# Sixteen-head values turned by VectorE's block transposes, and self-attention with scores 32 keys wide, in a two-layer latent transformer kernel

## The chip, the cores and the metric

The kernel runs on one core of a Trainium2 chip. The metric is the device time of one execution in microseconds; lower is better. The engines are named as in the profile: PE is TensorE's matrix multiplication and PEld its loading of weights, DVE is VectorE, ACT is ScalarE, POOL is GpSimd, SP is SyncE. Each has its own instruction queue and works it off in order; an instruction waits at the head of its queue until the semaphores that it needs have come up, and everything behind it waits too.

## The reference, cut to what matters

The input x has 128 sequences of 32 tokens with 256 features, and each sequence has a context of 257 rows. Six blocks follow one another, each of the form x = x + f(layernorm(x)):

```python
x = x + _L0_xattn_ref(_layernorm(x), ctx_1024, ...)   # one head, 257 context keys
x = x + _L0_attn_ref(_layernorm(x), ...)              # one head of 128, causal over the 32 tokens
x = x + _L0_ffn_ref(_layernorm(x), ...)               # quantised feed-forward, 256 -> 1024 -> 256
x = x + _L1_xattn_ref(_layernorm(x), ctx_1024, ...)   # 16 heads of 16, 257 context keys
x = x + _L1_attn_ref(_layernorm(x), ...)              # tokens at most 2 away
x = x + _L1_ffn_ref(_layernorm(x), ...)               # 8 experts, the best 2 for each token
```

Three of them matter here. The sixteen-head cross attention computes, for each sequence, softmax(q k) v for 16 heads with 32 queries and 257 keys, and multiplies the concatenated heads by an output matrix. The two self-attentions (causal in layer 0, a band of five tokens in layer 1) only ever combine tokens of one sequence of 32.

## The kernel before

A tile is 128 rows, that is four sequences of 32 tokens; there are 32 tiles. The first phase takes each tile through all six blocks up to the router. It is software-pipelined: a slot of the program holds, on each engine, the steps of up to nine tiles at different depths (`slot(s)` in each engine's block, with `at(s + 3, ...)` for a tile that is three behind in depth), and the order of the steps in a slot is written out by hand for every engine. The second phase runs the experts: 71 blocks of 128 gathered rows, each with 2 x 8 products up and 8 down. Some closing steps of the last two tiles stand between the first expert blocks.

The sixteen-head attention is the largest part of a slot. A unit is one sequence of a tile, so a slot has four units. For a unit, PE writes scores into PSUM banks 0 to 3 (`unit_scores`, L1246), DVE takes row maxima (`unit_max`, L1797), ACT takes exponentials and row sums (`unit_probs`, L1431), PE transposes the probabilities in the same four banks (`unit_probs_T`, L1254), ACT copies them out (L1435), and PE multiplies by the context (`values_of`, L1265) into bank `V{u}`. The next unit's scores wait for that copy, since they use the same banks. The rows of the V bank are (head within half, query), and its 64 columns hold four groups of 16 features.

What follows the values is the part that the change replaces. DVE adds the last key's product (`unit_own`, L825), then multiplies by a 0/1 selection of two halves that carries the reciprocal of the row sum (L827, 128 columns wide; the selection comes from POOL, `unit_select`, L1562). PE folds the rows with a constant matrix (`unit_fold`, L729), which also turns features to partitions. DVE copies the result from PSUM to the tile's transposed output (`unit_folded`, L832). `s1_out` multiplies that by the output matrix.

In both self-attentions PE computes scores for 128 queries against all 128 keys of a tile, and a mask 128 wide removes the keys of other sequences (`masked_max`, L812 and L814). ACT takes the exponential; PE transposes the probabilities (`s0_probs_T` L1178, `s1_probs_T` L777); ACT copies them out (L1387, L896); PE multiplies by the values (`s0_values` L1182, `s1_values` L782). In layer 0, DVE divides by the row sum ahead of the transpose (L1733). In layer 1 this is done behind the values (`s1_x5`, L863).

Two helpers of the waits appear below: `W_bank` names the last readers of the PSUM bank that a product is about to overwrite, and `f1_ok` counts units whose folded values are ready.

## Time and profile before

| quantity | value |
|---|---|
| median of 3 runs | 1440.78 us (1439.78 to 1440.86) |
| the profiled execution | 1438.83 us |
| span of its trace | 1436.9 us |
| granted TensorE clock, mean over the span | 0.989 |
| PE busy | 1383.0 us, 96% |
| PEld busy | 1181.8 us, 82% |
| DVE busy | 892.7 us, 62% |
| ACT busy | 839.2 us, 58% |
| POOL busy | 642.2 us, 45% |

The shares are averages over two phases with different limits: in the first, three engines are busy nearly all the time; in the second, DVE and ACT have little to do. Matmuls are pipelined and their ends are modelled, so records of PE overlap; the same holds for DVE and ACT, where an instruction's record can start before the one ahead has ended. The time that an instruction costs its queue is read from start to start.

### The profile page before, as it was taken

The numbers are of one execution on the slowest core, as the hardware profiler recorded it, in microseconds if no ns is written. First come the engines' busy times: TensorE is split into PE (matmuls) and PEld (weight loads), VectorE is DVE, ScalarE is ACT, GpSimd is POOL, SyncE is SP. The second block draws the span as 40 slices with busy tenths as digits, with TensorE's granted clock in tenths as the row PEclk, the third lists the DMA queues.
The fourth block names the chain that finished last, engine by engine and source line by source line (L and its number), as shares of the span: only waits on it lengthen the run. The fifth ranks groups of instructions, "written<-read, shape, count | busy, mean of one in ns | idle before, by whom it ended". The sixth has DMA issues, their size and how long they took to land. (4 is left out here: it accounts for less than half of the span.)

```text
span 1436.9 us, 51496 instructions
## 1 busy us (share of the span) xinstructions
PE 1383.0 (96%) x19614; PEld 1181.8 (82%) x19647; DVE 892.7 (62%) x3143; ACT 839.2 (58%) x2431; POOL 642.2 (45%) x1195
## 2 busy tenths in 40 slices
PE   8789999999999999999999988999999999999996
PEld 6467788878878788888887866899999999999996
DVE  5678989999999999999999985333111111111111
ACT  1588989889888898889888875331111111111110
POOL 1233444434455455454554543366544434444442
PEclk9899999999999999999999999999999999999999
DMA  9423433334334334343332233666666666665662
GB/s 326 152 72 95 123 105 106 119 94 117 105 113 116 102 102 120 107 121 101 105 113 87 62 130 114 227 177 180 180 182 182 191 183 182 181 182 178 181 181 58
DMA packets 91181, 199.49 MB, mean 139 GB/s; under 512 B 13568, under 2 KB 48128, under 8 KB 79840
## 3 DMA queue, kind: packets, MB, share of 16 engines
q1 hardware_dynamic: 72304, 174.68, 38.3%
q0 software_dynamic: 15680, 18.69, 7.3%
q10 hardware_dynamic: 2992, 3.28, 0.7%
q8 instruction: 141, 2.31, 0.6%
q14 instruction: 64, 0.52, 0.1%
HBM read 178.58 MB, written 18.29 MB: 137 GB/s over the span
## 5 line engine op out<-in xcount | busy, mean ns | idle before, releaser
L2177 ACT ACTIVATE heT<-ps 128x512 f32<-128x512 f32 x142 | 84.8, 598 | 411.9 <-PE ps L2099 382.7
L2099 PEld LDWEIGHTS ps<-xeT,w_block 128*128 128x128 f32 x2272 | 264.8, 192 | 3.6 <-issue 0.2
L2099 PE MATMUL ps<-xeT,w_block 128*128 128x128 f32 x2272 | 266.2, 275 | 0.0
L1431 ACT ACTIVATE x_prob<-ps,x_nmax 128x257 f32<-128x257 f32 x512 | 237.5, 473 | 46.5 <-DVE x_nmax L1797 41.9
L2086 PE MATMUL ps<-contexts,heT 128*128 x1136 | 257.6, 379 | 1.6 <-DVE ye L1984 1.6
L2086 PEld LDWEIGHTS ps<-contexts,heT 128*128 128x128 f32 x1136 | 210.1, 190 | 27.6 <-issue 1.9
L1797 DVE TENSOR_REDUCE x_nmax<-ps 128x2 f32<-128x514 f32 x256 | 169.0, 681 | 18.9 <-PE ps L1246 18.6
L1983 DVE COPY to_ix<-places 128x1 uint32 x71 | 10.9, 154 | 231.8 <-PE ps L2086 228.2
L1254 PE MATMUL ps<-constants,x_prob 128*128 128x128 f32 x1024 | 150.1, 280 | 4.3 <-ACT x_prob L1431 4.1
L1435 ACT ACTIVATE x_probT<-ps 128x512 f32<-128x512 f32 x256 | 148.2, 632 | 3.6 <-PE ps L1254 3.3
L2220 POOL TENSOR_TENSOR rt_hold<-constants 128x1 f32<-128x1 f32 x143 | 35.0, 244 | 227.2 <-DVE ye L1984 121.0
L1254 PEld LDWEIGHTS ps<-constants,x_prob 128*128 128x128 f32 x1024 | 115.5, 143 | 19.2 <-ACT x_prob L1431 14.0
L2226 POOL DMA_INDIRECT out<-ye,to_ix x71 | 113.0, 1592 | 28.5 <-issue 23.8
L1265 PEld LDWEIGHTS ps<-contexts,x_probT 128*32 128x32 f32 x8192 | 90.5, 110 | 31.4 <-ACT ffn_hidden L1400 11.8
L1431 ACT ACTIVATION_READ_ACCUMULATOR x_prob<-ps,x_nmax 128x1 f32 x512 | 103.2, 202 | 0.0
L1265 PE MATMUL ps<-contexts,x_probT 128*32 128x16 f32 x8192 | 93.9, 185 | 6.3 <-issue 5.9
L1246 PE MATMUL ps<-contexts,query_blocks 32*64 32x257 f32 x2048 | 89.4, 405 | 6.8 <-ACT x_probT L1435 4.8
L2002 DVE COPY xeT<-ps 128x256 f32<-128x256 f32 x71 | 30.1, 424 | 85.0 <-PE ps L2077 85.0
L2223 POOL DMA_INDIRECT xe<-xnorm,from_ix x69 | 69.2, 1003 | 22.5 <-issue 20.4
L1562 POOL TENSOR_TENSOR x_select<-constants,x_rinv 128x8 f32<-128x8 f32 x128 | 27.5, 215 | 107.7 <-DVE x_rinv L1801 107.7
L1557 POOL TENSOR_TENSOR x_lastv<-contexts,x_prob 128x64 f32<-128x64 f32 x128 | 40.6, 317 | 55.5 <-ACT x_prob L1431 55.0
L1246 PEld LDWEIGHTS ps<-contexts,query_blocks 32*64 32x64 f32 x2048 | 30.3, 131 | 41.9 <-ACT x_probT L1435 25.1
(287 smaller groups left out, 2940.2 us busy)
## 6 DMA issues: line engine op xcount, KB each, us to landing
w_block<-in_m_w SPq DMA_DIRECT2D x71, 1024.0 KB
contexts<-in_cT SPq DMA_DIRECT2D x112, 257.0 KB
contexts<-in_cn SPq DMA_DIRECT2D x112, 256.0 KB
contexts<-in_m_w SPq DMA_DIRECT2D x8, 1024.0 KB
contexts<-in_cT SPq DMA_DIRECT2D x4, 1028.0 KB
xin<-in_x SPq DMA_DIRECT2D x32, 128.0 KB, 2.1
lastq<-in_lastq SPq DMA_DIRECT2D x32, 128.0 KB, 2.2
contexts<-in_cn SPq DMA_DIRECT2D x4, 1024.0 KB
```

Of the source, the lines that this page charges most:

```text
L1246: i = mm(ps[h * HS:(h + 1) * HS, r, 0:KEYS], qblk[t % 2][r * GD:(r + 1) * GD, h, u, :, :].rearrange("p e q -> p (e q)"), cT[t % RING][r * ...
L1254: i = tr(ps[:, r, n * P:(n + 1) * P], p1[u % 2][:, r, n * P:(n + 1) * P], ident[:])
L1265: i = mm(b[rows_of, r * DH:(r + 1) * DH], p1T[u % 2][:, r, n, rows_of], cn[t % RING][:, u, n, lo:lo + DH], start=n == 0, stop=n == KT - 1)
L1431: A(p1[u % 2][:, r, :], ps[:, r, 0:KEYS], ACT.Exp, bias=nmax1[u % 2][:, r:r + 1], accum_out=rsum1[u % 2][:, r:r + 1]).then_inc(e1_ok.handl ...
L1435: A(p1T[u % 2][:, 2 * j:2 * j + 2].rearrange("p r k t -> p r (k t)"), ps[:, 2 * j:2 * j + 2, 0:KT * P], ACT.Copy).then_inc(t1_ok.handle, 1)
L1557: tt(lastv[u % 2][:].rearrange("p (r d) -> p r d", r=RG), lastk[t % RING][:, u, :].rearrange("p (r d) -> p r d", r=RG), p1[u % 2][:, :, KE ...
L1797: v_.tensor_reduce(nmax1[u % 2][:, 2 * j:2 * j + 2], ps[:, 2 * j:2 * j + 2, 0:KEYS], AX, ALU.max, negate=True).then_inc(m1_ok.handle, 1)
L2086: t = mm(ps[:, 3, 0:D], heT[b][:, k, :], w2[:, e, k, :], start=k == 0, stop=k == FK - 1)
L2099: t = mm(ps[:, half, at:at + P], w1[b][:, k, f * P:(f + 1) * P], xeT[b][:, k, :], start=k == 0, stop=k == H - 1)
L2177: A(heT[b][:, half * FK // 2:(half + 1) * FK // 2, :].rearrange("p k t -> p (k t)"), ps[:, half, :], ACT.Gelu).then_inc(heT_ok.handle, 1)
L2223: g.indirect_dma_start(xe[b][:], None, sources[round_of(u, n)], bass.IndirectOffsetOnAxis(ap=from_ix[b][:], axis=0)).then_inc(xe_in[b], 16)
L2226: g.indirect_dma_start(sums[round_of(u, n)], bass.IndirectOffsetOnAxis(ap=to_ix[b][:], axis=0), ye[b][:], None, compute_op=ALU.add).then_i ...
```

## The change

It has four parts.

1. Values of the sixteen heads. The columns of the value weights are put in another order on the host (`x1_wv`), so that 32x32 blocks turned in place give the wanted layout. The selection, the product with it and the fold are gone. DVE adds the last key (`unit_own`), POOL divides by the row sum (`unit_scaled`, 128x64), and DVE turns the 32x32 blocks of the result into the transposed output (`unit_turned`, one transpose, 128x64). `unit_values` of units 1 and 3 wait for other readers of their banks than before, since the fold's banks are no longer used.
2. Layer 0 self-attention. PE computes four 32x32 score products instead of one of 128x128. The mask, maximum and exponential are 32 columns wide. DVE multiplies by the reciprocal of the row sum and spreads the 32 columns over 128 under a block mask in one instruction, and turns the 32x32 blocks with a transpose of 128x128. PE's transpose and ACT's copy are gone.
3. Layer 1 self-attention. Eight 32x32 score products instead of two of 128x128, and again mask, maximum and exponential 32 wide. DVE turns the 128x32 probabilities and spreads them under the block mask (`s1_turned`). PE's transpose and ACT's copy are gone. `s1_out` now stands ahead of `s1_values` on PE.
4. Order. On POOL the steps `unit_scaled` stand near where `unit_select` stood, with the changes shown below.

The core of the diff:

```diff
         def s1_out(t):
             W(pe, f1_ok, t, NB)
-            W_bank(pe, (t - 1, (act_s["self1"], "probsT")))
...
-            product(bank(B["s1_v_scores"])[:, D:D + P], [(q1T[:, k, :], xnT["self1"][:, k, :]) for k in range(H)]).then_inc(pe_s["self1"].handle, 1)
-
-        def s1_probs_T(t):
-            W(pe, act_s["self1"], t, "probs")
-            W_bank(pe, (t + 1, (f1_ok, 3)))
-            tr(bank(B["s1_probs_T"])[:, 0:P], prob["self1"][:], ident[:]).then_inc(pe_s["self1"].handle, 1)
+            for k in range(H):
+                for b in range(NB):
+                    i = mm(bank(B["s1_v_scores"])[b * S:(b + 1) * S, D:D + S], q1T[:, k, b * S:(b + 1) * S], xnT["self1"][:, k, b * S:(b + 1) * S], start=k == 0, stop=k == H - 1)
+            i.then_inc(pe_s["self1"].handle, 1)
...
             W(dve, v1_ps, t, u + 1)
-            W(dve, sel_ok, t, u + 1)
+            W(dve, lv_ok, t, u + 1)
+            W_if(dve, before[0], n1_ok, before[1] + 1)
             v_.tensor_tensor(own[q][:], bank(B[f"V{u}"])[:, 0:OWN], lastv[q][:], ALU.add).then_inc(o1_ok.handle, 1)
-            W(dve, o1_ok, t, u + 1)
-            v_.tensor_tensor(om[q][:], own[q][:].rearrange("p (r d) -> p r d", r=RG).unsqueeze(1).broadcast_to([P, H, RG, DH]),
-                             select[q][:].unsqueeze(3).broadcast_to([P, H, RG, DH]), ALU.mult).then_inc(om_ok.handle, 1)
-
-        def unit_folded(t, u):
-            W(dve, f1_ps, t, u + 1)
-            v_.tensor_copy(outT[t % 2][:, :, u * S:(u + 1) * S], bank(B[f"f{u}"])[:, 0:HS].rearrange("p (e q) -> p e q", e=HG)).then_inc(f1_ok.handle, 1)
+
+        def unit_turned(t, u):
+            W(dve, n1_ok, t, u + 1)
+            v_.transpose(outT[t % 2][:, :, u * S:(u + 1) * S], scaled[u % 2][:].rearrange("p (j c) -> p j c", j=H)).then_inc(f1_ok.handle, 1)
...
+        def s1_turned(t):
+            W(dve, act_s["self1"], t, "probs")
+            v_.transpose(turned[:], prob["self1"][:]).then_inc(dve_s["self1"].handle, 1)
+            W(dve, dve_s["self1"], t, "turned")
+            v_.tensor_tensor(in_blocks(probT["self1"][:, 0, :]), turned[:].unsqueeze(1).broadcast_to([P, NB, S]), in_blocks(const["blocks"]), ALU.mult).then_inc(dve_s["self1"].handle, 1)
...
+        def unit_scaled(t, u):
+
+            q = u % 2
+            before = unit_before(t, u, 2)
+            W_if(pool, before[0], f1_ok, before[1] + 1)
+            W(pool, r1_ok, t, u + 1)
+            W(pool, o1_ok, t, u + 1)
+            tt(scaled[q][:].rearrange("p (r d) -> p r d", r=RG), own[q][:].rearrange("p (r d) -> p r d", r=RG),
+               rinv1[q][:].unsqueeze(2).broadcast_to([P, RG, DH]), ALU.mult).then_inc(n1_ok.handle, 1)
...
                 W(dve, dve_s["self0"], t, "inv")
-                v_.tensor_scalar(prob["self0"][:], prob["self0"][:], rinv["self0"][:], None, ALU.mult).then_inc(dve_s["self0"].handle, 1)
+                v_.scalar_tensor_tensor(in_blocks(spread[:]), prob["self0"][:].unsqueeze(1).broadcast_to([P, NB, S]), rinv["self0"][:], in_blocks(const["blocks"]), ALU.mult, ALU.mult).then_inc(dve_s["self0"].handle, 1)
+                W(dve, dve_s["self0"], t, "scaled")
+                v_.transpose(probT["self0"][:, 0, :], spread[:]).then_inc(dve_s["self0"].handle, 1)
```

The first place is on VectorE (DVE) in the last part of a slot, from the third unit's turned values to the row maxima of the next tile's second unit. The row `rt_rest` belongs to the router, `ffn_hidden` and `ffn_hq` to the feed-forward of another tile. Before:

```order
L832 COPY x1_outT<-ps 128x2x32
L812 SCALAR_TENSOR_TENSOR self1_masked<-ps,constants 128x128
L814 TENSOR_REDUCE self1_nmax<-self1_masked 128x1
L1760 TENSOR_SCALAR ffn_hidden<-ffn_hidden,ffn_qscale 128x1024
L1762 TENSOR_SCALAR ffn_hq<-ffn_hidden 128x1024
L1797 TENSOR_REDUCE x1_nmax1<-ps 128x2
L832 COPY x1_outT<-ps 128x2x32
L273 SCALAR_TENSOR_TENSOR rt_rest<-rt_hot,rt_shifted 128x32
L1797 TENSOR_REDUCE x1_nmax1<-ps 128x2
L818 RECIPROCAL self1_rinv<-self1_rsum 128x1
```

And now:

```order
L816 STREAM_TRANSPOSE x1_outT<-x1_scaled0 128x2x32
L797 SCALAR_TENSOR_TENSOR self1_masked<-ps,constants 128x32
L799 TENSOR_REDUCE self1_nmax<-self1_masked 128x1
L1742 TENSOR_SCALAR ffn_hidden<-ffn_hidden,ffn_qscale 128x1024
L1744 TENSOR_SCALAR ffn_hq<-ffn_hidden 128x1024
L1780 TENSOR_REDUCE x1_nmax1<-ps 128x2
L816 STREAM_TRANSPOSE x1_outT<-x1_scaled1 128x2x32
L843 STREAM_TRANSPOSE self1_prob_turned<-self1_prob 128x32
L845 TENSOR_TENSOR self1_probT<-self1_prob_turned,constants 128x128
L273 SCALAR_TENSOR_TENSOR rt_rest<-rt_hot,rt_shifted 128x32
L1780 TENSOR_REDUCE x1_nmax1<-ps 128x2
L803 RECIPROCAL self1_rinv<-self1_rsum 128x1
```

The two copies from PSUM have become transposes in SBUF, the mask is narrower, and two instructions have come in ahead of the second row maximum.

The second place is on GpSimd, at about the same time, from the bias of one tile to the reciprocal deviation of the layer 1 self-attention. Before:

```order
L915 TENSOR_TENSOR self0_x_bias<-x1_0,r_a0_bo 128x256
L1562 TENSOR_TENSOR x1_select1<-constants,x1_rinv1 128x8
L1557 TENSOR_TENSOR x1_lastv0<-contexts,x1_prob 128x64
L915 TENSOR_TENSOR x3_bias<-x3,r_x1_bo 128x256
L915 TENSOR_TENSOR self1_x_bias<-x4,r_a1_bv 128x256
L909 TENSOR_TENSOR router_var_eps<-router_moments,epsilon 128x1
L911 TENSOR_TENSOR router_rstd<-router_var_eps,minus_half 128x1
L1562 TENSOR_TENSOR x1_select0<-constants,x1_rinv0 128x8
L915 TENSOR_TENSOR cross0_x_bias<-xin3,r_x0_bv 128x256
L1557 TENSOR_TENSOR x1_lastv1<-contexts,x1_prob 128x64
```

And now:

```order
L904 TENSOR_TENSOR self0_x_bias<-x1_0,r_a0_bo 128x256
L924 TENSOR_TENSOR x1_scaled0<-x1_own0,x1_rinv0 128x64
L924 TENSOR_TENSOR x1_scaled1<-x1_own1,x1_rinv1 128x64
L1542 TENSOR_TENSOR x1_lastv0<-contexts,x1_prob 128x64
L904 TENSOR_TENSOR x3_bias<-x3,r_x1_bo 128x256
L904 TENSOR_TENSOR self1_x_bias<-x4,r_a1_bv 128x256
L898 TENSOR_TENSOR router_var_eps<-router_moments,epsilon 128x1
L900 TENSOR_TENSOR router_rstd<-router_var_eps,minus_half 128x1
L904 TENSOR_TENSOR cross0_x_bias<-xin3,r_x0_bv 128x256
L1542 TENSOR_TENSOR x1_lastv1<-contexts,x1_prob 128x64
```

Two products 128x64 stand where one of 128x8 stood, and the bias `cross0_x_bias` follows the router's `router_rstd` with nothing between them.

The third place is on TensorE, from the next tile's second scores to the hidden transposes of the feed-forward. Before:

```order
L1246 MATMUL ps<-contexts,query_blocks1 64x257 x8
L729 MATMUL ps<-constants,x1_own_half1 128x64
L777 MATMUL ps<-constants,self1_prob 128x128
L709 MATMUL ps<-self0_normT,w_a0_Wq_T 128x128 x2
L709 MATMUL ps<-self0_normT,w_a0_Wk_T 128x128 x2
L709 MATMUL ps<-w_a0_Wv_T,self0_normT 128x128 x2
L782 MATMUL ps<-self1_val,self1_probT 128x256
L709 MATMUL ps<-x1_W,x1_outT 128x128 x4
L1254 MATMUL ps<-constants,x1_prob 128x128 x8
```

And now:

```order
L1243 MATMUL ps<-contexts,query_blocks1 64x257 x8
L711 MATMUL ps<-self0_normT,w_a0_Wq_T 128x128 x2
L711 MATMUL ps<-self0_normT,w_a0_Wk_T 128x128 x2
L711 MATMUL ps<-w_a0_Wv_T,self0_normT 128x128 x2
L711 MATMUL ps<-x1_W,x1_outT 128x128 x4
L767 MATMUL ps<-self1_val,self1_probT 128x256
L1251 MATMUL ps<-constants,x1_prob 128x128 x8
```

The fold and the transpose are gone, and the output product has moved ahead of the values of the self-attention.

## Rows read from the trace of the kernel before

**Rows 1.** Windows of the trace: stretch, length, busy time and instructions per engine, clock, DMA
```profile
112.90:839.40 726.50, 715.63 (x13905) 582.67 (x13933) 671.50 (x2336) 645.40 (x1985) 353.47 (x763) 1.00 0.36 107
910.00:1437.00 527.00, 515.07 (x3543) 484.01 (x3541) 106.16 (x444) 92.34 (x153) 232.08 (x305) 0.99 0.61 172
```

**Rows 2.** DVE groups from 112.9 to 839.4 us: busy us, mean ns, idle before
```profile
L832 DVE COPY x_outT<-ps 128x64 f32<-128x64 f32 x112 | 24.6, 220 | 7.4 <-PE ps L729 7.2
L812 DVE SCALAR_TENSOR_TENSOR self_masked<-ps,constants 128x128 f32<-128x128 f32 x56 | 16.3, 290 | 5.7 <-issue 2.4 <-ACT self_val L888 2.3 <-PE ps L1173 0.6
L814 DVE TENSOR_REDUCE self_nmax<-self_masked 128x1 f32<-128x128 f32 x56 | 16.0, 286 | 1.9
L1733 DVE TENSOR_SCALAR self_prob<-self_prob,self_rinv 128x128 f32<-128x128 f32 x28 | 8.3, 295 | 1.0
L273 DVE SCALAR_TENSOR_TENSOR rt_rest<-rt_hot,rt_shifted 128x32 f32<-128x32 f32 x6 | 1.1, 182 | 0.0
L263 DVE TENSOR_REDUCE rt_top<-rt_key 128x4 f32<-128x32 f32 x6 | 1.1, 180 | 0.0
```

**Rows 3.** Waits from 112.9 to 839.4 us: total us, times, longest
```profile
POOL x_lastv L1557 <- ACT x_prob L1431: 40.0, 13, 3.6
ACT query_normT L1415 <- PE ps L1226: 32.2, 28, 1.2
ACT x_prob L1431 <- DVE x_nmax L1797: 31.7, 56, 1.2
PEld ps L1246 <- ACT x_probT L1435: 19.9, 59, 0.9
DVE x_nmax L1797 <- PE ps L1246: 10.6, 30, 0.4
DVE x_outT L832 <- PE ps L729: 7.2, 28, 0.7
```

**Rows 4.** DVE timeline, the fourth unit's addition and product: start, duration in us
```profile
407.22 0.22 DVE L825 TENSOR_TENSOR x_own<-ps,x_lastv 128x64 f32<-128x64 f32 x1
407.47 0.29 DVE L827 TENSOR_TENSOR x_own_half<-x_own,x_select 128x128 f32<-128x128 f32 x1
407.68 1.21 DVE L1750 TENSOR_REDUCE ffn_absmax<-ffn_hidden 128x1 f32<-128x1024 f32 x1
```

**Rows 5.** PE timeline around a fold, a change of tile shape and score products
```profile
404.00 0.33 PE L729 MATMUL ps<-constants,x_own_half 128*128 128x64 f32 x2
404.16 0.59 PE L709 MATMUL ps<-f,ffn_xqT 128*128 128x512 bf16 x2
404.69 0.69 PE L1246 MATMUL ps<-contexts,query_blocks 32*64 32x257 f32 x16
411.66 0.28 PE L777 MATMUL ps<-constants,self_prob 128*128 128x128 f32 x1
411.78 0.61 PE L709 MATMUL ps<-self_normT,w_a_Wq_T 128*128 128x128 f32 x4
416.75 0.47 PE L1173 MATMUL ps<-self_kT,self_qT 128*128 128x128 f32 x2
417.15 0.69 PE L1246 MATMUL ps<-contexts,query_blocks 32*64 32x257 f32 x16
```

**Rows 6.** ACT timeline around one of the two copies that go
```profile
420.59 0.29 ACT L1387 ACTIVATE self_probT<-ps 128x128 f32<-128x128 f32 x1
420.75 0.50 ACT L1431 ACTIVATE x_prob<-ps,x_nmax 128x257 f32<-128x257 f32 x1
```

**Rows 7.** Timelines of POOL and DVE, where work of both overlaps
```profile
414.92 0.82 POOL L915 TENSOR_TENSOR cross_x_bias<-xin,r_x_bv 128x256 f32<-128x256 f32 x1
415.18 0.60 DVE L288 TENSOR_TENSOR rt_key<-rt_key,constants 128x32 f32<-128x32 f32 x1
```

**Rows 8.** DVE timeline: the first unit's addition, and its copy after the fold
```profile
419.90 0.22 DVE L825 TENSOR_TENSOR x_own<-ps,x_lastv 128x64 f32<-128x64 f32 x1
422.25 0.23 DVE L832 COPY x_outT<-ps 128x64 f32<-128x64 f32 x1 [0.19 <-PE ps L729]
```

More of the change, by code:

```diff
@@ L544, in stack_phase @@
     val = {n: small(n, "val", D) for n in ATT[1:]}
-    masked = {n: small(n, "masked", P) for n in ATT[1:]}
+    masked = {n: small(n, "masked", S) for n in ATT[1:]}
+    spread = small("self0", "prob_spread", P)
+    turned = small("self1", "prob_turned", S)
     nmax = {n: small(n, "nmax") for n in ATT}
@@ L602, in stack_phase @@
         "cross0": ["normT", "q", "scores", "probsT", "values", "attT", "out"],
-        "self0": ["normT", "qkv", "scores", "probsT", "values", "out"],
+        "self0": ["normT", "qkv", "scores", "values", "out"],
         "ffn_in": ["inT"],
@@ L695, in at @@
         name = step.__name__
-        left = CLOSING.get(name, int(name in ("unit_own", "unit_fold", "unit_folded") and unit[0] >= 2))
+        left = CLOSING.get(name, int(name in ("unit_own", "unit_scaled", "unit_turned") and unit[0] >= 2))
         if 0 <= t < tiles - left:
@@ L1084, in setup_folds @@
                 t.then_inc(su_mm, 1)
[L1086 removed]
+            product, product_in_halves, route_counts, W_counts, s1_out, s1_norm_T, s1_q, s1_v_scores, s1_values, ro_norm_T, ro_logits = tensor_steps(pe)
             def c0_norm_T(t):
@@ L2030, in _ @@
             unit_own(tiles - 1, 3)
-            unit_folded(tiles - 1, 2)
+            unit_turned(tiles - 1, 2)
             s1_masked(tiles - 2)
-            unit_folded(tiles - 1, 3)
+            unit_turned(tiles - 1, 3)
             stage_from(2, 0)
+            s1_turned(tiles - 2)
             s1_inv(tiles - 2)
@@ L2048, in _ @@
             s1_masked(tiles - 1)
+            s1_turned(tiles - 1)
             s1_inv(tiles - 1)
@@ L2070, in _ @@
             mm = nc.tensor.matmul
-            product, product_in_halves, unit_fold, route_counts, W_counts, s1_out, s1_norm_T, s1_q, s1_v_scores, s1_probs_T, s1_values, ro_norm_T, ro_logits = tensor_steps(pe)
+            product, product_in_halves, route_counts, W_counts, s1_out, s1_norm_T, s1_q, s1_v_scores, s1_values, ro_norm_T, ro_logits = tensor_steps(pe)
             def rows_T(u, b):
```

160 lines of the change are left out of this document (67 added, 93 removed), and 3 rows, old and new, of the table B.

## The prediction, on record before the change was run

> **What bounds the kernel now.** I read the windows first, because the page's shares mix two phases. The stretch from 112.9 to 839.4 us [rows 1] holds 28 slots: the copy L832 has 112 records there, four in a slot [rows 2]. So a slot takes 726.5 / 28 = 25.95 us. Busy in it: PE 98%, DVE 92%, ACT 89%, POOL 49%. The last 527 us are the experts, where DVE and ACT are busy for a fifth of the time and PE for 98%. The change touches nothing of an expert block, so that stretch keeps its length whatever happens ahead of it.
>
> The waits of the same stretch come second [rows 3]. Per slot, DVE waits 10.6 / 28 = 0.38 us for PE's scores and 7.2 / 28 = 0.26 us for the fold; together about 0.6 us of 26. ACT waits 2.3 us, for PE's query transposes and DVE's maxima. PE waits 0.7 us for ACT's copies. The reader is to see a ring: scores on PE, maxima on DVE, exponentials on ACT, transposes on PE, copies on ACT, and then the next unit's scores in the same banks. Steps of other tiles fill each queue in between. DVE has the least slack, PE little more, ACT the most. So a shorter DVE queue is worth the most, as long as PE's shrinks as much and ACT can give up enough of its 2.3 us.
>
> **The change, part by part.** Costs of DVE are from start to start.
>
> *Units.* In [rows 4] the addition starts at 407.22, the product with the selection at 407.47, the next instruction at 407.68: 0.25 + 0.21 us. The 0.25 contains the wait for the addition's own result. An instruction that nobody waits for overlaps the next by 0.08 us (0.29 long, 0.21 to the next start), so alone the addition costs 0.22 - 0.08 = 0.14. Four units: 4 x (0.46 - 0.14) = 1.28 us less in a slot.
>
> *Transposes.* No row of before has one on DVE. I price them like a product. SCALAR_TENSOR_TENSOR takes 182 ns for 32 columns and 290 for 128 [rows 2], so about 1.1 ns a column and 217 ns for 64, against 220 for the PSUM copy that goes. The four `unit_turned` then cost nothing net. A slot transposes 416 columns (4 x 64 + 128 + 32). From below I bound them by half that slope, since an instruction with one input might stream faster: 0.23 us less. From above by double the slope: 0.46 us more. I take the middle, to which all rows of products are nearest. The Trainium skill (VectorE: DVE Perf Modes, The three transpose paths) gives 311 ns for 128x128 in bf16; by it the sum would be 0.02 us longer per slot. No row here shows it.
>
> *Narrow masks.* Mask and maximum go from 290 and 286 to 182 and 180 ns [rows 2]: 0.21 us, for two self-attentions 0.43 us less.
>
> *Layer 0 spread and transpose.* The product 128x128 (295 ns [rows 2], 0.21 to the next start) becomes a product with two inputs (0.29 + 0.03 for the wait behind it) and a transpose (0.21): 0.32 us more.
>
> *Layer 1 turn.* Transpose 128x32 (0.18 + 0.03) and product 128x128 (0.21): 0.42 us more, ahead of the second row maximum of the next unit, for which ACT's exponentials wait.
>
> DVE's sum is -1.28 - 0.43 + 0.32 + 0.42 = -0.97 us a slot.
>
> *PE.* A fold takes 0.16 us of the queue (404.00 to 404.16 [rows 5]), four 0.64. A transpose takes 0.12 (411.66 to 411.78), two 0.24. The layer 0 scores take 0.40 from start to the next product (416.75 to 417.15), those of layer 1, twice the records of the same shape at 0.11 to 0.12 each, about 0.44. The new ones are 8 and 16 records of 32 columns into four groups of output partitions. Sixteen records of 257 columns in small tiles need 0.62 us of queue at most (0.69 long [rows 5]), so the new ones get 0.1 and 0.2. A change of tile shape costs too: of the two L709 records at 404.16 the second starts 0.22 later, at 404.38, and L1246 starts at 404.69, 0.31 behind it instead of 0.22. That is 0.09 us for a change; layer 0 adds one and layer 1 two. The new scores take about 0.2 and 0.4 instead of 0.84. PE's sum: -0.64 - 0.24 - 0.24 = -1.1 us a slot, so PE follows DVE.
>
> The Trainium skill (TensorEngine Tiling (Array Packing), Key Properties) says that changing the tiling mode drains TensorE, which speaks against the small products. The trace shows a drain at 0.09 us. Were it a whole record (0.28) three times, PE's sum would be -0.55, and PE would set the slot at 0.4 us less than now instead of 0.9.
>
> *ACT.* A copy costs 0.16 us (420.59 to 420.75 [rows 6]). Two go, and two exponentials lose 96 columns, by DVE's slope 0.1 us each: -0.5. To follow DVE, ACT gives up 0.4 of its 2.3 us of waiting.
>
> *POOL.* Four products 128x64 replace four of 128x8. Here the trace speaks against the change. At 414.92 POOL starts a bias, and DVE's 32-column product at 415.18 takes 0.60 us [rows 7], where such a product takes 0.18 [rows 2]: 0.4 us lost. The new order puts that bias right behind the router's deviation, so that it can fall on layer 1's turn, which works in SBUF; and POOL's product for the second unit can fall on the normalisation behind that unit's addition. I bound this by 0 (no overlap) and 0.8 us (both hit) a slot and take 0.3. The Trainium skill (GPSIMD Engine Reference, Specifications) says that the SBUF interfaces are shared with VectorE, with contention for two-input and two-port instructions; the trace agrees.
>
> POOL's wait for the additions of the last two units stands where it waited for exponentials before (40.0 / 13 = 3.1 us each time [rows 3]), so what is behind it in the queue is not later. The closest pair of addition and turned unit on DVE is 2.35 us apart (419.90 and 422.25 [rows 8]), against a product of POOL of well under 1 us. No new wait.
>
> *Moved products.* `s1_out` now runs ahead of `s1_values`, so `s1_x5` gets its values about an output product later, and `s1_x` its sum earlier. DVE has the turn, a maximum of 0.6 us and a normalisation between. No cost.
>
> **The sum.** DVE -0.97, the wait for the fold -0.26, contention +0.3: 0.9 us a slot, 28 slots, 25 us. Ahead of 112.9 and behind 839.4 us lie parts of about four more slots, which I price at 0.75 us each: 3 us. Against the profiled execution 1438.8 - 28 = 1410.6 us. It lies 1.95 us below the median of the runs, so against the median 1412.5 us.
>
> **The rivals.** The forecast, 0.9 us a slot, has a chance of 0.49.
>
> First, more: ring and queues close up together, so that ACT's and PE's savings count beside DVE's and nothing collides. With the bound of no contention DVE alone gives 0.97 + 0.26 = 1.23 us a slot: 1440.8 - 35 - 4 = 1402 us. For it: all three engines wait for one another in [rows 3]. Against it: their savings lie beside each other in time as often as behind each other. Chance 0.2.
>
> Second, less, from DVE: transposes at their upper bound (+0.46) and contention at its own (0.8 instead of 0.3) leave nothing of the 0.9; halfway, at 0.4 us a slot, it is 1440.8 - 11 - 2 = 1428 us. For it: the 0.60 in [rows 7]. Against it: the additions that go were as exposed as the products that come. Chance 0.15.
>
> Third, less, from ACT: its queue loses only 0.5 us, and if its waits are latency of the ring and not slack, the slot loses no more than that: 1440.8 - 14 - 2 = 1425 us. Against it: the waits are in two places of the slot and both are for engines that get shorter. Chance 0.1.
>
> Fourth, slower: a block transpose is dear. The 0.9 us are used up when each of the 416 columns costs 2.2 ns more than the 1.1, that is from 3.3 ns. At 5 ns it is 0.7 us more a slot, 1460 us. Against it: operations of quite different kinds have the same slope in [rows 2] (product 1.1, maximum 1.1). Chance 0.04.
>
> Fifth, no change: DVE's queue is shorter, but what arrives sets the pace. The 0.6 us that DVE waits now would then grow to 1.5 a slot. Against it: PE at 98% loses 1.1 us too. Chance 0.02.
>
> **How the numbers follow.** The range takes in the first three rivals with the bounds of what they price: 1396 to 1431 (from 1.4 to 0.3 us a slot). A measurement of this kernel can tell 0.2% (2.9 us) from no change. Faster: the forecast and the first three rivals, 0.94. Same: the fifth, 0.02. Slower: the fourth, 0.04.
>
> **What would show it.** In the changed kernel's trace: the spacing of unit scores four apart is near 25.0 us; transposes 128x64 take 200 to 250 ns and 128x128 about 290; the narrow masks 180; there is no wait of DVE for a fold; the new layer 0 scores take PE under 0.3 us; DVE's normalisation behind the second unit's addition stays at 0.41 or doubles (contention); ACT's waits shrink by 0.4 us a slot. The prediction is wrong if the transposes' slope is above 2 ns a column, if POOL's bias stretches the 128x128 product beyond 0.5 us, or if a new wait for POOL's scaled values shows up on DVE.

## The result, and the profile after

The changed kernel is slower: 1457.21 us median of 4 runs (1453.08 to 1459.9) against 1440.82 us (1439.78 to 1443.4), ratio 1.0106 with a 95% interval of [1.0081, 1.013]. Its profiled execution took 1456.48 us. The head of its page, and the row of the queue that brings PE's instructions (packets, MB, share):

```profile
span 1454.7 us, 51945 instructions
PE 1365.7 (94%) x19870; PEld 1136.4 (78%) x19903; DVE 870.6 (60%) x3111; ACT 823.6 (57%) x2367; POOL 653.1 (45%) x1195
q8 instruction: 142, 2.33, 0.6%
```

Every engine but POOL is busy for less time than before, and the span is 17.8 us longer. What went must have come back as waiting. Windows of the changed kernel, from the start of a slot (unit 3's scores, L1243) to the start of another, columns as in [rows 1]:

```profile
139.40:267.40 128.00, 124.17 (x2519) 95.23 (x2524) 114.21 (x379) 111.92 (x344) 58.87 (x131) 1.00 0.38 110
423.00:749.60 326.60, 303.32 (x6072) 234.91 (x6084) 282.00 (x1006) 271.87 (x831) 165.64 (x339) 0.99 0.34 104
749.60:855.30 105.70, 98.99 (x2003) 75.53 (x2007) 95.56 (x351) 89.83 (x271) 54.03 (x109) 1.00 0.29 94
```

And of the kernel before, the same slots:

```profile
138.40:266.40 128.00, 127.09 (x2479) 103.32 (x2484) 116.27 (x385) 114.79 (x354) 57.36 (x130) 1.00 0.37 110
422.90:734.00 311.10, 307.55 (x5977) 251.06 (x5989) 289.73 (x1018) 277.56 (x855) 161.36 (x340) 1.00 0.37 110
734.00:839.40 105.40, 102.17 (x1973) 82.44 (x1977) 97.80 (x356) 91.55 (x279) 54.21 (x111) 1.00 0.29 94
```

The reader is to see two results. Slots 2 to 6 (128.0 us, five slots) are exactly as long as before, 25.60 us each: no gain where nothing disturbs. Slots 13 to 24 (twelve slots) took 311.1 us and take 326.6: a loss of 15.5 us, nearly the whole difference. The rest of the balance: start +1.2, the other early slots -1.1, slots 25 to 28 +0.3, the last two slots +3.5, what is behind -1.6; together 17.8 us.

The operations of the change on DVE, as groups from 112.9 to 839.4 us (busy us, mean ns | idle before):

```profile
L816 DVE STREAM_TRANSPOSE x_outT<-x_scaled 128x64 f32<-128x64 f32 x110 | 25.3, 230 | 0.0
L812 DVE TENSOR_TENSOR x_own<-ps,x_lastv 128x64 f32<-128x64 f32 x111 | 21.2, 206 | 6.9 <-PE ps L1262 6.8
L845 DVE TENSOR_TENSOR self_probT<-self_prob_turned,constants 128x128 f32<-128x128 f32 x27 | 13.9, 513 | 0.9
L797 DVE SCALAR_TENSOR_TENSOR self_masked<-ps,constants 128x32 f32<-128x32 f32 x54 | 10.2, 189 | 33.3 <-ACT self_val L881 18.1 <-issue 14.8
L1713 DVE SCALAR_TENSOR_TENSOR self_prob_spread<-self_prob,self_rinv,constants 128x128 f32<-128x128 f32 x27 | 9.5, 352 | 1.0
L1715 DVE STREAM_TRANSPOSE self_probT<-self_prob_spread 128x128 f32<-128x128 f32 x27 | 8.4, 312 | 0.9
```

The block transposes cost what the prediction gave them. The new thing is L797: DVE idles 33.3 us ahead of the narrow masks.

**A slot without a stall.** Waits of ACT from 139.4 to 267.4 us, five slots (total us, times, longest):

```profile
ACT x_prob L1418 <- DVE x_nmax L1780: 8.9, 15, 0.9
ACT query_normT L1402 <- PE ps L1223: 5.8, 5, 1.2
```

In the kernel before, from 138.4 to 266.4 us:

```profile
ACT query_normT L1415 <- PE ps L1226: 5.8, 5, 1.2
ACT x_prob L1431 <- DVE x_nmax L1797: 5.5, 10, 0.8
```

ACT's busy time fell by 2.87 us in these five slots (114.79 to 111.92), and its waiting rose by 3.4. Its queue runs through the whole slot with these waits alone. Where they come from is seen on DVE, in the slot that starts at 241.8 us:

```profile
254.75 0.19 DVE L797 SCALAR_TENSOR_TENSOR self_masked<-ps,constants 128x32 f32<-128x32 f32 x1 [0.82 <-ACT self_val L881]
254.98 0.19 DVE L799 TENSOR_REDUCE self_nmax<-self_masked 128x1 f32<-128x32 f32 x1
255.08 0.77 DVE L1742 TENSOR_SCALAR ffn_hidden<-ffn_hidden,ffn_qscale 128x1024 f32<-128x1024 f32 x1
255.88 1.10 DVE L1744 TENSOR_SCALAR ffn_hq<-ffn_hidden 128x1024 bf16<-128x1024 f32 x1
256.90 0.68 DVE L1780 TENSOR_REDUCE x_nmax<-ps 128x2 f32<-128x514 f32 x1
257.50 0.23 DVE L816 STREAM_TRANSPOSE x_outT<-x_scaled 128x64 f32<-128x64 f32 x1
257.66 0.16 DVE L843 STREAM_TRANSPOSE self_prob_turned<-self_prob 128x32 f32<-128x32 f32 x1
257.86 0.64 DVE L845 TENSOR_TENSOR self_probT<-self_prob_turned,constants 128x128 f32<-128x128 f32 x1
258.42 0.68 DVE L1780 TENSOR_REDUCE x_nmax<-ps 128x2 f32<-128x514 f32 x1
```

DVE reaches the mask early and waits 0.82 us for ACT's copy of layer 1's values, which stands where it stood before: the saving ahead of it is lost there. Behind it layer 1's turn (257.66 to 258.42, 0.76 us) stands ahead of the second row maximum, and ACT waits for that one too, 0.41 us, where it had waited once for this unit. The product of the turn takes 0.64 us with POOL's bias running beside it; in the slots where nothing 128x256 on POOL overlaps it, it takes 0.29:

```profile
257.62 0.73 POOL L904 TENSOR_TENSOR cross_x_bias<-xin,r_x_bv 128x256 f32<-128x256 f32 x1
```

Why ACT waits although it has work in its queue is seen at the start of a slot, here the one at 190.6 us:

```profile
189.91 0.64 ACT L1422 ACTIVATE x_probT<-ps 128x512 f32<-128x512 f32 x1
191.71 0.39 ACT L1402 ACTIVATE query_normT<-ps 128x256 f32<-128x256 f32 x1 [1.15 <-PE ps L1223]
```

PE's unit scores may start only behind this copy, at 190.61; they and the query transposes behind them take until ACT's next step. So the 1.15 us are the way from ACT's own copy through PE and back, and no shorter queue of DVE changes them.

**A slot with a stall.** PE in the slot that starts at 450.1 us, which takes 28.4 us:

```profile
458.54 1.29 PE L1262 MATMUL ps<-contexts,x_probT 128*32 128x16 f32 x125
461.48 0.24 PE L1262 MATMUL ps<-contexts,x_probT 128*32 128x16 f32 x3 [1.65 <-issue]
```

It stops three products before the end of the values products of units 2 and 3, and no semaphore holds it ("issue"). In the transfers from 459.0 to 460.3 us there is one packet of the instruction queue:

```profile
q8 instruction: 1, 0.02, 5.5%
```

The packet starts at 459.06 and takes 1.15 us; PE goes on at 461.48, 2.4 us behind its start. By the page, 142 such packets bring 2.33 MB, so PE's code comes in pieces of 16 KB. Counting PE's records in the trace (loads of weights, products, waits), I find one piece per 256 records. A slot has 1029 records in the trace of the changed kernel and 1020 in that of the kernel before, so the borders of the pieces move through the slot: earlier by 5 records from slot to slot in the one, later by 4 in the other, and some slots have 9 or 13 records more. I number them by the records ahead of a slot's start, modulo 256. In the changed kernel this count is 47 to 67 in slots 2 to 7, 72 to 102 in slots 8 to 12, and 107 to 192 in slots 13 to 24.

The clock is touched as well: behind two of the stalls in slots 13 to 24 (those that end at 490.0 and 572.5 us) the granted clock stood at the lower of its two levels, 1.2 GHz, for 3.4 us.

### The profile page after: what moved, and what is told of

Read it like the earlier page. It is cut to its first block and busy times, and to the rows that moved or that the text cites. A ratio compares the mean times of both kernels' runs of the same rounds, so it can differ in the third digit from the quotient of the medians.

```text
span 1454.7 us, 51945 instructions
## 1 busy us (share of the span) xinstructions
PE 1365.7 (94%) x19870; PEld 1136.4 (78%) x19903; DVE 870.6 (60%) x3111; ACT 823.6 (57%) x2367; POOL 653.1 (45%) x1195
## 3 DMA queue, kind: packets, MB, share of 16 engines
q8 instruction: 142, 2.33, 0.6%
## 5 line engine op out<-in xcount | busy, mean ns | idle before, releaser
L1251 PE MATMUL ps<-constants,x_prob 128*128 128x128 f32 x1024 | 157.6, 284 | 14.0 <-ACT x_prob L1418 12.3
L1422 ACT ACTIVATE x_probT<-ps 128x512 f32<-128x512 f32 x256 | 147.9, 626 | 11.1 <-PE ps L1251 10.0
L1251 PEld LDWEIGHTS ps<-constants,x_prob 128*128 128x128 f32 x1024 | 119.3, 145 | 34.9 <-ACT x_prob L1418 27.8
L2208 POOL DMA_INDIRECT out<-ye,to_ix x71 | 113.0, 1592 | 28.4 <-issue 23.9
L924 POOL TENSOR_TENSOR x_scaled<-x_own,x_rinv 128x64 f32<-128x64 f32 x128 | 37.0, 297 | 177.5 <-DVE x_own L812 169.1
L1243 PE MATMUL ps<-contexts,query_blocks 32*64 32x257 f32 x2048 | 89.0, 403 | 16.0 <-ACT x_probT L1422 13.8
L2205 POOL DMA_INDIRECT xe<-xnorm,from_ix x69 | 69.2, 1003 | 22.5 <-issue 20.3
L1243 PEld LDWEIGHTS ps<-contexts,query_blocks 32*64 32x64 f32 x2048 | 30.3, 130 | 50.1 <-ACT x_probT L1422 33.5
## 6 DMA issues: line engine op xcount, KB each, us to landing
contexts<-in_cn SPq DMA_DIRECT2D x112, 256.0 KB
xin<-in_x SPq DMA_DIRECT2D x32, 128.0 KB, 2.1
lastq<-in_lastq SPq DMA_DIRECT2D x32, 128.0 KB, 2.2
```

Source lines behind the costliest of these rows:

```text
L1243: i = mm(ps[h * HS:(h + 1) * HS, r, 0:KEYS], qblk[t % 2][r * GD:(r + 1) * GD, h, u, :, :].rearrange("p e q -> p (e q)"), cT[t % RING][r * ...
L1251: i = tr(ps[:, r, n * P:(n + 1) * P], p1[u % 2][:, r, n * P:(n + 1) * P], ident[:])
L1422: A(p1T[u % 2][:, 2 * j:2 * j + 2].rearrange("p r k t -> p r (k t)"), ps[:, 2 * j:2 * j + 2, 0:KT * P], ACT.Copy).then_inc(t1_ok.handle, 1)
L2205: g.indirect_dma_start(xe[b][:], None, sources[round_of(u, n)], bass.IndirectOffsetOnAxis(ap=from_ix[b][:], axis=0)).then_inc(xe_in[b], 16)
L2208: g.indirect_dma_start(sums[round_of(u, n)], bass.IndirectOffsetOnAxis(ap=to_ix[b][:], axis=0), ye[b][:], None, compute_op=ALU.add).then_i ...
```

## The experiments: does the place of PE's code matter?

Two theories stood after the comparison. A: pieces of code that come late at a bad place of the slot cost the 15 us. B: the change's own work does (POOL beside DVE, new waits). The test shifts the code by records that do nothing, ahead of the first tile, and leaves all else. Each ratio below is against the kernel before, timed beside the run; its median lies between 1440.8 and 1443.5 us from one group of runs to another, so runs of different groups are best compared by their ratios. The first form:

```diff
             keep_busy(13)
+            for _ in range(56):
+                mm(ps[:, 3, 0:1], zero[:, 0:P], zero[:, 0:1], start=True, stop=True)
```

**56 products in the changed kernel.** 

> The changed kernel with 56 extra products of one column (112 records on PE) ahead of the first tile, where PE waits for the first loads. Nothing else differs. Theory A: the 20 us that the changed kernel loses between 423 and 907 us come from where the boundaries of the loaded pieces of PE's code fall in a slot (one piece per 256 records, a slot has 1029). They then fall 112 records earlier in the program, the slots of 27 to 29 us go, and the time comes to 1432 to 1440 us. Theory B: the loss is the work itself (POOL's products beside DVE's, waits for the turned probabilities): the same as the changed kernel within 3 us, 1457.

1473.46 us, ratio 1.0216 [1.0193, 1.0238].

**96 products in the changed kernel.** 

> The changed kernel with 96 extra products of one column (192 records on PE) at the same place. Theory A: the first half of the tiles runs in slots of 25.6 to 26 us, the second half gets the stalls that the changed kernel has in slots 13 to 19, shifted to later slots: 1440 to 1455 us, with a stall inside the block of values products in other slots than before. Theory B: 1457 as the changed kernel.

1481.71 us, 1.029 [1.0256, 1.0325].

**72 products in the kernel before.** 

> The kernel before with 72 extra products of one column (144 records on PE) at the same place. Theory A: the kernel before has 1020 records in a slot, so its boundaries hardly move from slot to slot; the shift puts them where the changed kernel stalls, in nearly all slots: 1455 to 1490 us, slots of 26.5 to 28.5 us. Theory B: 1441 as before, within 3 us.

1461.29 us, 1.0135 [1.0118, 1.0152].

All three expectations missed, for two reasons that the traces show. Each product left four records on PE, not two, so the shifts were 224, 384 and 288 records. And the products delayed the first tile by 21, 36 and 28 us. With the delay set aside the slots are informative: in the kernel with 96 products slots 13 to 24 have counts of 235 to 255 and 4 to 64 and take 26.03 us each, against 27.22 without them; with 56 products the counts are 75 to 160 and they take 27.07.

The second form uses small products (64 by 16, four records each), 28 of them for 112 records:

```diff
+            for i in range(28):
+                mm(ps[i % H * HS:(i % H + 1) * HS, 3, 0:DH], zero[:, 0:HS], zero[:, 0:DH], start=True, stop=True)
```

**28 small products in the changed kernel.** 

> The changed kernel with 28 small products (64 by 16, of zeros, 112 records on PE) ahead of the first tile, so that PE's code is shifted by 112 records. The products of 128 by 1 of the first four runs had four records each and delayed the first tile by 21 to 36 us; these should delay it by less than 3. Theory A (pieces of PE's code come late where their boundary falls ahead of the values products): a slot that starts with 72 to 165 records (of 256, counted in the trace) is long, and this shift takes all slots but the last few out of that range: slots 13 to 24 of 25.6 to 26.2 us instead of 25.8 to 28.7, in all 12 to 20 us less than the changed kernel, 1437 to 1446 us. Theory B (work and contention): 1457 us plus the delay of the first tile.

1450.64 us, 1.0069 [1.0046, 1.0092]. Slots 13 to 24 take 26.03 us each, as expected; but slots 2 to 5, with counts of 159 to 169, take 28.0 to 29.5, so the bad range reached further than I had it. Not all of that is code: each of the four has a gap of 2.1 us from start to start, and at the end of each gap or up to 1.3 us behind it the granted clock fell to 1.2 GHz for 3.4 to 6.8 us (mean 0.92 from 142.4 to 256.0 us). What such a fall costs is seen in the next kernel, where one of the slots with a gap has it and takes 28.8 us, while the others up to slot 24 take 27.0 to 27.8.

**35 in the kernel before.** 

> The kernel before with 35 such products (140 records on PE), which by theory A puts all its slots from 3 to 28 into the long range: slots of 26.5 to 28 us instead of 25.7 to 26.3, and 1465 to 1490 us. Theory B: 1441 to 1445 us.

1479.39 us, 1.0277 [1.0235, 1.0318]: 38 us lost by 140 records that do nothing. Waits of PE from 439.8 to 767.8 us, slots 13 to 24:

```profile
PEld ps L1267 <- issue: 20.9, 12, 2.1
PE ps L1267 <- issue: 19.7, 12, 2.0
```

Each of the twelve slots stalls in the values products, about 1.7 us. In the whole run there are 26 such gaps, and PE goes on 2.2 to 2.8 us behind the start of a packet of code every time.

**32 in the changed kernel.** 

> The changed kernel with 32 small products of zeros (128 records on PE) ahead of the first tile: 16 records more than the kernel with 28. By the count of records at each slot's start, slots 2 to 5, which were 28 us long with 28 products, leave the long range, and slots 25 to 28 stay at its other edge. Theory A: 8 to 12 us less than with 28 products, 1438 to 1443 us, and slots 2 to 24 on average 25.9 us, as the kernel before. Rival: the long slots of a run are set by something else than the count, and the time stays at 1448 to 1452 us.

1446.87 us, 1.0035 [1.002, 1.0051]. One gap is left, in slot 3.

**8 in the kernel before.** 

> The kernel before with 8 such products (32 records on PE), by the same count its best place: slots 7 to 9 and 14 of 26.3 to 26.8 us become 25.7 us: 2 to 5 us less than before, 1436 to 1439 us. With it stands how the change compares at the best place of each: theory A gives a difference of less than 5 us between this kernel and the changed one with 32 products. Rival: no effect, 1441 us.

1435.09 us, 0.9954 [0.9936, 0.9973], with no such gap left. But it and the changed kernel are 11.8 us apart, not less than 5: this half of the expectation missed, and the end of the text comes back to it.

| kernel | count in slots 13 to 24 | mean slot, 13 to 24 |
|---|---|---|
| before, 8 small products | 27 to 37 | 25.88 us |
| before | 226 to 245 | 25.93 us |
| changed, 28 small products | 219 to 249, then 7 to 48 | 26.03 us |
| changed, 32 small products | 250, then 9 to 90 | 26.05 us |
| changed, 56 products | 75 to 160 | 27.07 us |
| changed | 107 to 192 | 27.22 us |
| before, 35 small products | 110 to 129 | 27.33 us |

Theory A holds, in both kernels and both directions: counts of about 100 to 170 cost 1.0 to 1.5 us a slot. The counts have one flaw. Most of the traces lack the record of one product in each slot (the changed kernel has 19,902 loads of weights and 19,870 products); in the table only the kernels with 32 and with 8 small products lack none, so in slots 13 to 24 the counts of the other rows are too low by 16 to 28. With this set right the gaps fall on one place: all 26 in the kernel with 35 small products, and all five of over 0.9 us in the values products of the changed kernel, stand 193 or 194 records behind a multiple of 256. A border of a piece does that; work and contention, which know nothing of such a count, would not. The Trainium skill (Runtime: NRT & Kernel Launch, Instruction fetch mechanics) says that code is fetched in 16 KiB blocks of 256 instructions and that crossing a boundary is mostly hidden. The trace agrees with the sizes; it doesn't agree that it is hidden here, where 256 records of the values products pass in 1.3 us and the next piece needs 2.2 us or more.

## The experiments: why no slot got shorter

**ReLU for GELU in the changed kernel with 32 small products.** It takes ACT's two table loads (1.28 us each) away and computes another function in the feed-forward. The second half of the hidden rows has the same edit.

```diff
-A(hid[:, 0:FF // 2], bank(B["ff_up0"]), ACT.Gelu, scale=dq[:, 0:1])
+A(hid[:, 0:FF // 2], bank(B["ff_up0"]), ACT.Relu, scale=dq[:, 0:1])
```

> a_code128 with ReLU in place of GELU in the feed-forward of the tiles, which takes two table loads of 1.28 us out of ACT's queue in each slot and nothing from another engine. Theory D (ACT's own queue, with the ring's latency where it waits, sets the slot, and DVE's and PE's savings lie in their slack): the slot shrinks by 0.5 us or more, up to DVE's queue: 24.3 to 25.3 us, 1400 to 1430 us. Rival (DVE sets the pace, as the prediction had it): ACT's waits grow by 2.5 us and the slot stays at 25.6 to 25.9 us, 1440 us.

1424.9 us, 0.9892 [0.9867, 0.9917]. Slots 4 to 7 take 24.78 us instead of 25.58. So 0.80 of the 2.56 us came back; the rest became waiting. In 102.3 us from 195.0 us on, ACT now waits 4.0 us for PE's products into the hidden rows, where it hadn't waited, and 10.6 us for the maxima instead of 7.1.

**The absolute maximum over 128 of 1024 columns, in the same kernel.** It takes 1 us from DVE and computes another scale.

```diff
-row_scale("ffn", t, 1, hid)
+row_scale("ffn", t, 1, hid[:, 0:P])
```

> a_code128 with the absolute maximum of the feed-forward's hidden rows taken over 128 of the 1024 columns, which takes 1.0 us out of DVE's queue in each slot (the scale is then another, the work behind it the same). Theory D (ACT's queue and the ring set the slot, DVE has slack): 25.4 to 25.6 us in slots 1 to 7, less than 0.2 us off, 1440 to 1447 us. Rival (DVE sets the pace, as predicted): 0.6 to 1.0 us off each slot, 1420 to 1430 us.

1442.77 us, 0.9994 [0.9978, 1.0009]. Slots 4 to 7 take 25.60 us, unchanged. The waits of DVE from 195.0 to 297.3 us, four slots:

```profile
DVE self_masked L797 <- ACT self_val L881: 7.0, 4, 1.8
```

The microsecond went into the wait for ACT's copy: 1.8 us a slot instead of 0.8. Theory D holds: in these slots ACT's queue with the ring's latency sets the length, and what DVE alone saves ahead of that copy is lost. Its 0.4% less in the ratio must lie outside these slots; slots 13 to 24 show 1.6 us of it (25.92 us each), and for the rest the profiled executions don't tell, since in this one slot 3 takes 28.1 us instead of 25.75, with a fall of the clock behind its gap.

**The turn behind the second row maximum.** Two kernels, with 56 large and with 28 small products:

```diff
-                at(s - 1, s1_turned)
                 routing(s - 1, 5)
                 at(s + 1, unit_max, 1, 1)
+                at(s - 1, s1_turned)
...
-                at(s - 1, s1_values)
                 at(s + 1, unit_probs_T, 1, 0)
+                at(s - 1, s1_values)
```

> The changed kernel with the 56 extra products, and the turn of layer 1's probabilities behind the second row maximum of the next unit on DVE instead of ahead of it; on PE the values product of layer 1 stands behind the next transposes instead of ahead. Theory C: in slots without a code stall the turn (0.9 us on DVE ahead of the maximum for which ACT's exponentials wait) is what takes back the saving: 0.3 us a slot less than the kernel with the 56 products alone, 8 to 10 us in all. Rival: ACT's chain ends elsewhere in the slot (its wait for the query transposes stays as long), and the time is the same within 3 us.

1475.95 us, 1.0236 [1.0194, 1.0277].

> a_code112 with the turn of layer 1's probabilities behind the next unit's second row maximum on DVE, and layer 1's values product behind the next transposes on PE. In the run with the 56 products the early slots took 25.12 to 25.30 us with this order, against 25.57. Theory C (the turn stands ahead of the maximum for which ACT waits, and takes back the saving): 25.1 to 25.3 us in all slots without a late piece of code, 8 to 10 us less than a_code112. Rival: later slots are set by what arrives, and it gains 2 us only.

1451.69 us, 1.0081 [1.0054, 1.0108]. In both, slots without a stall take 25.1 to 25.5 us up to slot 7, close to what was expected, and most later ones without a stall 26.1 to 26.8. So nothing is left of it in the whole, and both expectations missed in the time.

**Layer 1's mask between the two roundings of the hidden rows.** `s1_masked` goes from ahead of `ff_quantise_hidden` to between its two instructions. The kernel that ran also has the turn and the values product moved as in the runs above, against what its expectation says, so the run to compare it with is the one with 28 small products and the turn moved (1.0081). 

> a_code112 with layer 1's mask and maximum between the two roundings of the feed-forward's hidden rows on DVE, instead of ahead of both; the turn stays where the change put it. In the changed kernel DVE waits there 0.8 us for ACT's copy of layer 1's values. If that wait is a part of what takes back the saving, the row maximum of unit 1 starts 0.6 us earlier and the slot is 0.2 to 0.5 us shorter: 5 to 12 us less than a_code112. Rival: layer 1's exponential waits longer on ACT for the later maximum, and the slot stays or grows by up to 0.5 us.

1454.85 us, 1.0095 [1.0061, 1.0128]: a miss. Slots 6 to 8 took 25.2 to 25.5 us, as with the turn alone (25.3 to 26.0), and from slot 12 on they alternate between 25.7 and 27.0. What the mask's place does with the turn left where it was, no run shows.

**The turn's order, and layer 1's sum later on DVE.** `s1_x5` goes behind `s1_x` and `s1_moments`. 

> a_code128 with the turn of layer 1's probabilities behind the second row maximum on DVE, the values product behind the next transposes on PE, and layer 1's sum behind the next tile's sum and statistics on DVE (in the run with 28 products DVE waited 0.5 us a slot for that values product). Theory C (the turn's place takes back the saving): 25.2 to 25.4 us in slots 1 to 7 and 25.5 to 25.9 us in later ones, 5 to 12 us less than a_code128, which would beat both kernels. Rival: slots with the routing's operations on DVE are set by DVE's queue, and nothing is gained in them: 2 us less than a_code128.

1440.46 us, 0.9988 [0.9976, 1.0001]. Slots 4 to 7 take 25.1 us: 0.5 us a slot came back, as theory C has it, by order alone, and ACT's wait for the maxima fell by as much (5.4 us in four slots instead of 7.1). In slots 12 to 25 they take 25.7 to 27.3. It is the best form of the change that still computes the same, level with the kernel before and 5 us above that kernel's well placed form.

## The experiments: the slots from 13 on

In them DVE also carries the routing, and POOL writes table entries by indirect transfers.

**The indirect writes first on POOL.** `scatter_behind(s, s + 1, 3)` goes ahead of `unit_scaled` 2 and 3. 

> a_code128 with POOL's two indirect writes of table entries ahead of its products for units 2 and 3, as the kernel before has them ahead of its neighbours; in a_code128 they start 1.0 us later in the slot (11.1 instead of 10.1 us behind unit 3's scores), because POOL waits for DVE's additions first. Theory E: that lateness is why ACT's copies behind unit 0's exponentials lose 0.8 us in the slots from 14 on, and those slots get 0.2 to 0.4 us shorter: 1440 to 1444 us, 3 to 6 us less than a_code128. Rival: ACT's delay there has another cause, or the transposed unit 2 comes later on DVE and eats it: the same within 2 us.

1447.23 us, 1.0027 [1.0015, 1.0039]: the same as without it (1.0035) within the intervals. Slots 13 to 24 became longer: 26.35 us instead of 26.05.

**The same with the turn's order.** 

> Both orders together: the turn behind the second row maximum (which took slots 1 to 11 from 25.6 to 25.1 us) and the indirect writes first on POOL. Theory E: the slots from 14 on come from 26.2 to 25.6 us or less, and the time to 1428 to 1435 us, which beats both kernels. Rival: 1440 us as with the turn moved alone.

1444.27 us, 1.0006 [0.9993, 1.0018]: no better than the turn's order alone (0.9988).

**The kernel before with these writes later.** They wait for `o1_ok` instead of `v1_ps`. 

> The kernel before with 8 small products, and POOL's first pair of indirect writes waiting for DVE's addition of the last unit instead of PE's products of it, which is 0.8 us later. Nothing else differs. Theory E: the slots from 14 on get 0.2 to 0.5 us longer, with the gap in ACT's copies behind unit 0's exponentials: 3 to 8 us more than the kernel with 8 products, 1438 to 1443 us. Rival: 1435 us, unchanged, as POOL has slack.

1435.11 us, 0.9936 [0.992, 0.9951]; its slots 13 to 24 took 25.71 us, 0.16 less than with the writes early. Theory E falls in both directions. In the changed kernel with the writes first, ACT looks like this in the slot at 558.2 us:

```profile
570.34 0.21 ACT L1420 ACTIVATION_READ_ACCUMULATOR x_prob<-ps,x_nmax 128x1 f32 x1
571.19 0.38 ACT L1341 ACTIVATE cross_normT<-ps 128x256 f32<-128x256 f32 x1 [0.64 <-PE ps L1093]
```

PE's transposes L1093 start 11.1 us behind the slot's start, as in slots 1 to 11, but by the trace's semaphore updates their signal comes at 13.0 instead of 11.5. With 32 small products alone it comes at 12.4 to 12.5 in most of the slots from 13 on, so the moment of the writes does move it. In the kernel before it comes at 11.6 in most slots. What stands ahead of them on PE is new: the 16 small records of layer 1's scores.

**Layer 1's scores, mask and exponential 128 wide, turned by one block transpose; six zero products beside `s1_out` keep the record count.** Off its own 32 keys a row's probabilities are zero, so blocks are enough:

```diff
-            for k in range(H):
-                for b in range(NB):
-                    i = mm(bank(B["s1_v_scores"])[b * S:(b + 1) * S, D:D + S], ...)
+            product(bank(B["s1_v_scores"])[:, D:D + P], [(q1T[:, k, :], xnT["self1"][:, k, :]) for k in range(H)])
...
-            v_.tensor_tensor(in_blocks(probT["self1"][:, 0, :]), turned[:]..., ALU.mult)
+            v_.transpose(probT["self1"][:, 0, :], prob["self1"][:])
```

> a_code128 with layer 1's scores as one product 128 keys wide, its mask, maximum and exponential 128 wide as in the kernel before, and the turn by one block transpose of 128 columns (the probabilities outside a row's block are zero, so no spread is needed). Six products of zeros beside the output product keep PE's record count of a slot. In the slots from 13 on PE's completion signals behind the 16 small products of layer 1's scores came 1.0 to 1.7 us late in the changed kernel (12.5 to 13.2 us behind unit 3's scores), and on time (11.6) in the kernel before. Theory F: the small products are at fault: the signals come at 11.5 to 11.7 us again, the slots from 13 on take 25.6 to 25.9 us, and the time comes to 1436 to 1442 us. Rival: something else of the change (POOL's or DVE's order) is at fault: signals late as before, and 1446 us or more, since mask and maximum are 0.2 us longer.

1451.24 us, 1.0065 [1.0043, 1.0087].

> The same with the turn behind the next unit's second row maximum, the values product behind the next transposes and layer 1's sum behind the next tile's sum and statistics (the order that took slots 1 to 11 to 25.1 us). If theory F and theory C both hold, 25.1 to 25.3 us in the slots up to 12 and 25.4 to 25.8 in later ones: 1425 to 1434 us, which beats the kernel before and its shifted form (1435). Rival: the late slots stay at 26.2 us and the time at 1440 us.

1447.95 us, 1.005 [1.0025, 1.0075]. The signals come at 11.53 us in every slot up to 23 in both kernels, so the late ones do hang on the small products. But slots 13 to 24 still take 26.0 and 25.9 us, and with the turn's order slots 4 to 7 take 25.70, not 25.1. So half of theory F holds and the half that matters for the time does not. The likely cause of the 25.70, read from the trace and not tested alone: mask and maximum of 128 columns stand on DVE between ACT's copy of the values and the row maximum that ACT waits for next, and that wait reaches 1.11 us, against 0.91 with 32 columns; over four slots the waits for maxima are 6.9 us instead of 5.4.

## Why the prediction was wrong

- **The costs on DVE** were mostly right one by one. Transposes of 64 columns: 230 ns against 217 priced; of 128: 312 against 290; the masks 189 and 186 against 182 and 180; an addition alone 0.13 us (244.75 to 244.88) against 0.14. The spread and transpose cost 0.41 us more instead of 0.32. The turn cost 0.76 instead of 0.42, and its product 513 ns on average, above the 500 that the prediction named as a sign of being wrong. DVE's busy time fell by 0.41 us a slot. What is missing is contention with POOL, taken at 0.3 us and bounded by 0.8: beside the 0.35 us on the turn's product (0.64 instead of 0.29), the rounding of the feed-forward's input (L1742, 128x256) takes 0.70 us instead of 0.36 next to POOL's query blocks, and the two roundings of the hidden rows took 1.25 and 0.69 and take 0.77 and 1.10. By these rows I estimate 0.6 us a slot. Since DVE doesn't set the slot here, it cost nothing that was measured.
- **The step that failed** is the one from DVE's queue to the slot: "DVE has the least slack", and of ACT "To follow DVE, ACT gives up 0.4 of its 2.3 us of waiting". ACT has the most waiting [rows 3], but not slack: its waits are the time that the ring needs behind ACT's own copies, which the run with ReLU and the one with the shorter absolute maximum bear out: 2.56 us off ACT gave 0.80 a slot, 1.0 off DVE gave nothing. The wait for the query transposes stayed at 1.15 us. ACT lost 0.57 us of work, and the wait for the maxima rose by 0.68, behind a turn put ahead of one of them. The third rival had the mechanism, but priced it as a gain of 0.5 us; the turn's place took that too. Measured: 0.00 us a slot instead of 0.9, or 28 us of the miss of 45 (1457.2 against 1412.5). What spoke against the third rival, that both waits are for engines that get shorter, was no argument: the work that ACT waits for did not get shorter.
- **What was not in it at all** is the code of PE. The prediction read the change as 1.1 us less work on PE and did not count its records, 1020 to 1029 in a slot. Of the miss, 10 us are this (1457.2 to 1446.9 us with 32 small products); slots 13 to 24 of the profiled executions show 14 us. About 7 us of the miss are left without a cause.
- **POOL.** "What is behind it in the queue is not later" was wrong: the indirect writes start 1.0 us later (11.1 instead of 10.1 us). In no run did it cost anything that could be told from the noise.
- **The rivals.** The only one that ended slower had a dear block transpose, and the transposes cost what was priced: that the kernel came out slower was foreseen by none for the right reason.

The kernel before with 8 small products (0.9954), or with its writes later as well (0.9936), beats both kernels.

Open: with their code well placed the changed kernel has 1446.9 us and the one before 1435.1, though in the profiled executions (1441.85 and 1435.48) only 6.4 us of span lie between them: 2.1 in slots 13 to 24, 1.7 in slots 25 to 28, 3.0 in the last two, and 0.5 less in the rest together. Why neither the better order nor the prompt signals shorten the slots that also carry the routing isn't settled.

## What to carry to other kernels

The engine with the most waiting can be the one that sets the pace, when each of its waits is the way round a ring that starts at its own instruction; take work off one engine at a time to find out before a change is priced. Work moved to an engine with slack must not stand ahead of what the pacing engine waits for. In a long unrolled program a change of the instruction count is a change of its own: compare kernels at several shifts of the code before a per cent is put down to the edit.

## What the runs showed of the hardware

140 records of no use ahead of the first tile made a kernel 2.7% slower, and 32 made it 0.5% faster. PE stopped where a piece of 256 records ended within a dense run of small products (128 products in 1.3 us) and went on 2.2 to 2.8 us behind the start of the packet that brings the next. A product of 128x128 weights with one column is not small: 56 of them took 20.3 us ahead of the first tile, 0.36 us each, and while they ran the granted clock fell: 0.52 in the stretch from 20 to 40 us, so nearly all of it at the lower of the two levels, 1.2 GHz, against 1.00 in the same stretch without them.

A product 128x128 of two operands in SBUF took DVE 0.29 us alone or beside POOL's work on one column, and 0.64 beside an addition 128x256 on POOL.
